# Stage 1 of a fused attention and expert kernel: root steps divided between tiles 2 and 3, one chunk of statistics in another buffer, the first store of turned rows ahead of three loads

## The reference, cut to what matters

```python
mod = (silu(c) @ wmod)                        # six rows of 256: sa, ca, ga, sb, cb, gb
h = layernorm(x) * (1 + ca) + sa              # mean and variance of each token's 256 values
x_in = concat(mem, h)                         # 64 memory rows ahead of 4096 tokens
out_swa = swa(x_in, wq, wk, wv, wo)           # 4 heads, window 128
# loss = 0.5 * sum((mlp(x_in) - out_swa)**2); grads of w1, b1, w2, b2
# new = (1 - alpha) * old - theta * grad
out_mem = mlp(new, x_in)
x = x + ga * (sigmoid(out_swa @ lin1.T) * out_swa + sigmoid(out_mem @ lin2.T) * out_mem)[:, 64:]
h = layernorm(x) * (1 + cb) + sb
x = x + gb * (shared_expert(h) + top8_of_64_experts(h))
```

## Time and profile before

| | before |
|---|---|
| median of three runs | 1840.76 us |
| the profiled execution's own time | 1840.37 us |
| its span | 1838.2 us |
| PE busy | 1794.2 us (98%) |
| DVE busy | 1214.8 us (66%) |
| ACT busy | 947.9 us (52%) |
| POOL busy | 935.5 us (51%) |
| mean granted TensorE clock | 0.993 |

### The profile page before, as it was taken

The page is one execution under the profiler, slowest core; times in us unless marked ns, Lnnn a source line. Parts: engine busy times, 40 slices in busy tenths (PEclk is TensorE's granted clock), DMA queues, the critical chain, the costliest instruction groups (busy, mean ns, idle before and its releaser), DMA issues.

```text
span 1838.2 us, 35720 instructions
## 1 busy us (share of the span) xinstructions
PE 1794.2 (98%) x12168; PEld 1578.6 (86%) x12168; DVE 1214.8 (66%) x2253; ACT 947.9 (52%) x1792; POOL 935.5 (51%) x699
## 2 busy tenths in 40 slices
PE   7999999999999999999999999999999999999995
PEld 5788888888888887788788887889999999999995
DVE  7977777777777776766677668644555555555552
ACT  7666666666666665634545444343444434444341
POOL 6565666656666664046566666554233323332234
PEclk9999999999999999999999999999999999999998
DMA  6211111111111102220111103167898888888884
GB/s 239 69 39 36 38 37 35 38 35 35 55 39 35 39 28 81 70 74 17 47 46 47 47 12 109 39 227 254 291 286 288 283 279 281 289 289 283 284 278 96
DMA packets 141023, 234.16 MB, mean 127 GB/s; under 512 B 24757, under 2 KB 88972, under 8 KB 140817
## 3 DMA queue, kind: packets, MB, share of 16 engines
q1 hardware_dynamic: 116368, 220.50, 35.0%
q0 software_dynamic: 24576, 12.69, 4.6%
HBM read 194.58 MB, written 78.45 MB: 149 GB/s over the span
## 4 chain that ended last, share of the span: by engine, by line
PE 53%; DMA 3%; issue 1%; DVE 1%; POOL 0%; ACT 0%; SPq 0%; POOLq 0%; DVEq 0%; ACTq 0%
PE bank L86 26%; PE bank L2048 22%; PE bank L1312 4%; DMA out_rows<-c_y_rest,c_token_rest 2%; DMA c_w<-in_e1T 1%; PE bank L2270 1%; PE bank L1811 1%; DMA slots<-last_row,last_index 1%; POOL out_rows L2222 0%; POOL slots L2007 0%; PE bank L2281 0%; SPq L2104 0%; DVE c_y_rest L2189 0%; DVE early L1690 0%; POOLq L2356 0%
## 5 line engine op out<-in xcount | busy, mean ns | idle before, releaser
L2048 PE MATMUL bank<-c_xT,c_w 128*128 128x160 f32 x3072 | 429.9, 299 | 3.7 <-DMA c_w<-in_e1T 3.0
L2048 PEld LDWEIGHTS bank<-c_xT,c_w 128*128 128x128 f32 x3072 | 419.3, 190 | 5.0 <-DMA c_w<-in_e1T 3.4
L2007 POOL DMA_INDIRECT slots<-b_row,b_index x224 | 251.2, 1121 | 194.3 <-issue 116.4
L2222 POOL DMA_INDIRECT out_rows<-c_y,c_x x64 | 100.1, 1564 | 376.2 <-DMA out_rows<-c_y_rest,c_token_rest 275.1
L2170 DVE TENSOR_TENSOR c_gT<-bank,c_sil 128x480 f32<-128x480 f32 x128 | 84.2, 658 | 212.0 <-PE bank L2048 212.0
L2138 ACT CAST c_gTs_high<-c_gT 128x384 fp32r<-128x384 f32 x128 | 65.6, 513 | 135.3 <-DVE c_gT L2170 135.3
L2131 ACT ACTIVATE c_sil<-bank 128x480 f32<-128x480 f32 x128 | 73.1, 571 | 110.7 <-PE bank L2048 110.2
L2163 DVE TENSOR_TENSOR c_gTs_low<-c_gT,c_gTs_high 128x384 fp32r<-128x384 f32 x128 | 71.6, 560 | 74.8 <-ACT c_gTs_high L2138 74.8
L485 POOL TENSOR_TENSOR last_row<-last_row,a_e 128x256 f32<-128x256 f32 x33 | 53.5, 1620 | 124.5 <-DVE a_e L783 124.5
L86 PE MATMUL bank<-c_w2s_high,c_gTs_high 128*128 128x256 f32 x384 | 114.0, 297 | 0.9 <-DVE c_gTs_low L2163 0.9
L86 PE MATMUL bank<-c_w2s_high,c_gTs_low 128*128 128x256 f32 x384 | 106.9, 278 | 0.0
(11 more groups left out here) (346 smaller groups left out, 5451.0 us busy)
## 6 DMA issues: line engine op xcount, KB each, us to landing
c_w<-in_e1T SPq DMA_DIRECT2D x64, 1536.0 KB, 7.0
c_w<-in_e2T SPq DMA_DIRECT2D x48, 768.0 KB, 9.0
early<-in_e2T SPq DMA_DIRECT2D x16, 768.0 KB, 8.7
slots<-a_fill SPq DMA_DIRECT2D x16, 642.0 KB, 3.9
c_x<-slots SPq DMA_DIRECT2D x64, 160.5 KB, 8.6
a_x_in<-in_x SPq DMA_DIRECT2D x32, 128.0 KB, 2.0
xT_tiles<-a_xT SPq DMA_DIRECT2D x32, 128.0 KB, 1.7
swaT_tiles<-a_oT SPq DMA_DIRECT2D x32, 128.0 KB
```

What stands on the lines that cost most here:

```text
L2007: pool.indirect_dma_start(out=T["slots"], out_offset=bass.IndirectOffsetOnAxis(ap=index[:, t, k:k + 1], axis=0), in_=row[:, t, :], in_offs ...
L2048: return nc.tensor.matmul(out, lhsT, rhs, start=first, stop=last, skip_group_check=True)
L2222: pool.indirect_dma_start(out=T["out"], out_offset=bass.IndirectOffsetOnAxis(ap=token, axis=0), in_=rows, in_offset=None, bounds_check=las ...
```

## The change

- The wqk load and the cond load change places on SP.
- Chunk 4 goes to raw[2] instead of raw[1], chunk 6 to raw[3] instead of raw[2]; chunks 5, 6 and 7 thus share raw[3].
- SP loads chunk 1 alone before it stores tile 1's turned rows. Then come chunk 2, the two biases, step 1, chunk 3, chunk 4 (after `mod_mm` 3), chunk 5, step 2, chunk 6 (after `stats` 6) and chunk 7 (after `stats` 7), and only then the fills.
- ACT makes dz's high part of tile 0 in tile 1 ahead of h's high part, and no longer waits for five chunks' statistics.
- DVE in tile 1 does grad_z ahead of hidden_low and grad_z_low ahead of statistics(4).
- The twelve root steps of chunks 1 to 7 are cut otherwise: steps 0 to 5 behind statistics(7) in tile 2, steps 6 to 11 in tile 3 behind the reciprocal and the first of four gathers.

```diff
@@ -248,7 +248,7 @@
         wv_raw = h[:, 0:DC * D].rearrange("p (k n) -> p k n", k=DC)
 
         x_pre = [a.rearrange("p (t d) -> p t d", t=TPC)
-                 for a in (dz_raw[1], h_raw[0], h_raw[1], dz_sum[:], raw[1], dz_raw[1], dz_raw[0], dz_raw[1])]
+                 for a in (dz_raw[1], h_raw[0], h_raw[1], dz_sum[:], dz_raw[0], dz_raw[1], dz_raw[1], dz_raw[1])]
 
         def bank(b, n=CH):
             return psum[b][:, 0:n]
@@ -304,8 +304,8 @@
                 sp.dma_start(x_pre[c], x_chunks[c]).then_inc(S(f"x_pre{c}"), 16)
 
             sp.dma_start(x_in[0][P - MEM:P, :], T["mem"]).then_inc(S("mem_in"), 16)
+            sp.dma_start(wqk_raw, T["wqkT"]).then_inc(S("wqk_in"), 16)
             sp.dma_start(cond[:], T["c"]).then_inc(S("cond_in"), 16)
-            sp.dma_start(wqk_raw, T["wqkT"]).then_inc(S("wqk_in"), 16)
             load_chunk(0)
             for k in range(DC):
                 sp.dma_start(dW1T[:, k, :], T["w1T"][:, k, :]).then_inc(S(f"w1_in{k}"), 16)
@@ -325,12 +325,7 @@
             sp.wait_ge(S("xm"), 1)
             sp.dma_start(x_in[0][:], x_rows[P:2 * P, :]).then_inc(S("x_in0"), 16)
             sp.dma_start(dW2[:], T["w2n"]).then_inc(S("w2n_in"), 16)
-            for c in range(1, 4):
-                load_chunk(c)
-            sp.wait_ge(S("stats"), 1)
-            for name, into in (("b2c", b2c), ("b1c", b1c)):
-                sp.dma_start(into[:], T[name]).then_inc(S("small_in"), 16)
-
+            load_chunk(1)
             def step(n, p):
 
                 sp.wait_ge(S("xn"), n)
@@ -356,16 +351,20 @@
                                  fill[0:rows, half, :].unsqueeze(1).to_broadcast([rows, CLEARED, ROW]))\
                         .then_inc(S("slots_out"), 16)
 
+            keep_xT(1)
+            load_chunk(2)
+            for name, into in (("b2c", b2c), ("b1c", b1c)):
+                sp.dma_start(into[:], T[name]).then_inc(S("small_in"), 16)
+            step(1, 1)
+            load_chunk(3)
+            sp.wait_ge(S("mod_mm"), 3)
+            load_chunk(4)
+            sp.wait_ge(S("stats"), 1)
             load_chunk(5)
-            keep_xT(1)
-            sp.wait_ge(S("mod_mm"), 2)
-            load_chunk(4)
-            step(1, 1)
-            sp.wait_ge(S("mod_mm"), 3)
-            load_chunk(6)
             step(2, 0)
-            sp.wait_ge(S("stats"), 6)
-            load_chunk(7)
+            for c in (6, 7):
+                sp.wait_ge(S("stats"), c)
+                load_chunk(c)
             sp.wait_ge(S("fill"), 1)
             for half, rows in enumerate((P, CAP_B)):
                 sp.dma_start(T["out"][TOKENS + half * P:TOKENS + half * P + rows, :], fill[0:rows, half, 0:D])\
@@ -548,7 +547,6 @@
                     wait_past(act, S("dW_mm"), 4 * m - 4 * pm)
                 if not known(m, 1):
                     act.wait_ge(S("mod_mm"), 3)
-                    act.wait_ge(S("stats"), 5)
                 elif not known(m, 2):
                     act.wait_ge(S("stats"), CHUNKS)
                 for g in range(2):
@@ -652,14 +650,13 @@
                     turned(2, 0)
                 elif ahead(n):
                     turned(n + 2, p)
-                if known(n, 3):
+                if known(n, 1) and not (known(n, 2) and not known(n, 3)):
                     dz_high(n - 1, 1 - p)
                 if known(n, 1):
                     hidden_high(n, p)
                 if known(n, 1) and not known(n, 2):
                     act.wait_ge(S("w2n_low"), 4)
                     kept(dW2)
-                    dz_high(0, 0)
                 act.wait_ge(S("swa_mm"), n + 1)
                 wait_past(act, S("eT_mm"), n)
                 act.copy(swa[:], psum[7][:, D:2 * D]).then_inc(S("swa"), 1)
@@ -834,8 +831,6 @@
                     if known(n, 3) and not known(n, 4):
                         grad_z_low(1, 1)
                     turned_error_low(n - 1)
-                    if known(n, 3) and not known(n, 4):
-                        deviations(1, range(1, CHUNKS), range(5))
 
                 seen = slice(P - MEM if first else 0, P)
                 chosen = own[:, seen].unsqueeze(1).to_broadcast([P, DC, P - seen.start])
@@ -860,8 +855,6 @@
                     error_low(0, 0)
                 if known(n, 2) and not known(n, 3):
                     statistics(5)
-                if known(n, 3) and not known(n, 4):
-                    deviations(1, range(1, CHUNKS), range(5, RSQRT_OPS))
                 dve.wait_ge(S("prob_exp"), n + 1)
                 wait_past(dve, S("prob"), n)
                 dve.reciprocal(prec, psums).then_inc(S("prec"), 1)
@@ -876,8 +869,8 @@
                     modulate(1, 1)
                     part_prob(0, 0)
                 elif not known(n, 2):
+                    grad_z(0)
                     hidden_low(0, 0)
-                    grad_z(0)
                     hidden(1)
                     modulate(3, 1)
                     part_prob(1, 1)
@@ -886,7 +879,12 @@
                         dve.wait_ge(S("kept"), 1)
                     elif not known(n, 4):
                         dve.wait_ge(S("kept"), 2)
-                    gather_dW(n - 2, dW1T if p else dW2, (1, 2, 3, 4))
+                    if known(n, 3) and not known(n, 4):
+                        gather_dW(1, dW1T, (1, 2, 3, 4), (0,))
+                        deviations(1, range(1, CHUNKS), range(6, RSQRT_OPS))
+                        gather_dW(1, dW1T, (1, 2, 3, 4), (1, 2, 3))
+                    else:
+                        gather_dW(n - 2, dW1T if p else dW2, (1, 2, 3, 4))
                     if ahead(n):
                         modulate(n + 2, p)
                     part_prob(n, p)
@@ -920,10 +918,11 @@
                     dve.wait_ge(S("b2row"), 1)
                     dve.wait_ge(S("rates"), 1)
                 elif not known(n, 2):
+                    grad_z_low(0, 0)
                     statistics(4)
-                    grad_z_low(0, 0)
                 elif not known(n, 3):
                     statistics(7)
+                    deviations(1, range(1, CHUNKS), range(6))
                 else:
                     grad_z_low(n - 1, 1 - p)
```

## The result

The changed kernel takes 1846.47 us (median of 7 runs, 1844.04 to 1848.97) where the kernel before took 1840.92 beside it (7 runs, 1838.13 to 1841.71). The ratio is 1.0031, 95% interval [1.0019, 1.0043]: slower by 5.5 us. The forecast was 1841.9, a loss of 1.5 us in the profiled execution, with a range of 1837.4 to 1845.5; the median lies 1.0 us above the range. A later repeat (f1_again) gave 1845.54 us, ratio 1.0028 [1.0017, 1.0039]. The profiled execution took 1844.72 us (span 1842.5), 4.35 more than that of before.

A forecast was written before the change was run, and what follows sets the result against it. PE, busy 98% of the span, bounds the kernel, with holes only up to tile 3. DVE's +3.6 us, less 1.9 gained earlier and 0.2 of PE slack, gives +1.5 on 1840.4: 1841.9 us, range 1837.4 to 1845.5.

The forecast's parts named there:

- Up to chunk 6's statistics everything is thus 0.3 + 1.2 + 0.4 = 1.9 us earlier: Start to tile 2: gains of start, store and tile 1's reordering carry through, so these statistics start at 67.5 us.
- from reciprocal to hT low: Tile 3 on DVE: 8.1 us instead of 6.15, from seven added short steps and POOL's L459; hT low at 95.6.
- The new wait: Tile 2: DVE waits 3.5 us for chunk 7, issued only after chunk 6's statistics and landing 4.4 us later.
- the first meeting: Tile 3: DVE's dz low stands behind POOL's dz sum, costing 2.3 us, and is ready at 83.9 us.
- signs of being right: Expected in the profile: L509 without store wait, DMA wait in tile 2, root steps at 0.22 us, L770 behind POOL's L440.
- Start: First loads: wqk ahead of cond gains 0.3 us, between a gain of 0.6 and a loss of 0.6.
- Store: Tile 1: the first store, ahead of three loads, lands by 27 us, so PE gains its 1.2 us wait.
- The swap: Tile 1: grad_z ahead of hidden_low speeds POOL's product, but PE still needs h: 0, up to 0.9 us.
- (a): Tile 3: DVE gets its place ahead of POOL, no meeting, 2.4 us less: 1839.5 us; chance 0.20.
- (c): Tiles 2 and 3: quick chunk 7 load (3.1 us) and no meeting, 1838.2 us, at best 1837.4; chance 0.14.
- (b): Tile 2: chunk 7 lands late with the fills, up to 8.0 us after issue, 1845.5 us; chance 0.16.
- (d): Tile 1: the store still lands after chunk 2, losing its 1.2 us gain, 1843.1 us; chance 0.08.

The follow-up runs named there:

- f1_again: The changed kernel once more, unaltered, as a repeat: 1845.54 us, ratio 1.0028 to the kernel before.
- e9: The kernel before with only SP's new order (first store ahead of the chunk loads, fills last), chunks alternating between two buffers: 1837.94 us, ratio 0.9982.
- e8: e4 with all root steps back at their places in the kernel before, ahead of tile 3's picks and reciprocal: 1838.11 us, ratio 0.9987.
- e4: The changed kernel with chunk 6 back in dz_raw[0], hidden_low ahead of grad_z in tile 1 and cond loaded ahead of wqk: 1838.24 us, ratio 0.9990.
- f2: The changed kernel with PE's idle times in tiles 1 and 3 filled with products nobody reads: 1843.3 us, ratio 1.0014.
- e2: The changed kernel with hidden_low ahead of grad_z again in tile 1: 1844.14 us, ratio 1.0022.
- f4: The changed kernel with root steps 6 to 11 and the offset ahead of tile 3's reciprocal: 1843.19 us, ratio 1.0014.
- e5: e4 with root steps 6 to 11 and the offset ahead of tile 3's reciprocal instead of between its gathers: 1835.67 us, ratio 0.9970.
- f3: The kernel before with one number changed, chunk 7's load issued when chunk 6's statistics are done, not chunk 5's: 1842.36 us, ratio 1.0013.
- e7: The changed kernel with POOL's dz sum of tile 1 made to wait for dz low, so DVE goes first: 1845.03 us, ratio 1.0022.

## Why the prediction was wrong

Two steps failed. "Up to chunk 6's statistics everything is thus 0.3 + 1.2 + 0.4 = 1.9 us earlier": in the profiled execution it was 0.2 later, by the order of the first loads and by a fall of PE's clock. And "from reciprocal to hT low" took 10.0 us instead of 8.1, by a second meeting with POOL. The new wait and the first meeting, the core of the forecast, came out. All its signs of being right came too: none of them looked at when chunk 6's statistics begin or at what stands behind the reciprocal.

Point by point, with the steps as the prediction has them:

- **Start, "I take a gain of 0.3": wrong in sign.** S is 0.67 longer. Among profiles of kernels with the same start S spreads over 1.3 to 1.6 us; over the ten with cond behind wqk its mean is 21.4, over the eight with cond first 20.9: a cost of about 0.5. I had named this case ("a loss of 0.6 if cond's delay passes through") and chose the other, because DVE's statistics row 7.25 seemed to be the next step. It was not: q low waits for PE's products, and they begin at 6.14 behind ACT (5.79 before, behind the load of wqk).
- **Store, 1.2, and dz_high, 0.4: nearly right.** e9's A is 1.4 shorter, and e8 and e4, which have the other edits of tile 1 but the swap, are 0.25 and 0.44 shorter still.
- **The swap, "0, and up to 0.9": the order costs 0, its effect on the clock was missing.** With it and no long fall A is 32.67 (f1) and 32.68 (f2), without it 32.71 (e2). But it moves PE's idle time, to 1.05 and 1.85 us where the earlier trace rows and the trace of before have 1.72, 0.78 and 0.89. In all eight profiles with the swap and without filling in tile 1 the clock fell there, in five of them to 0.50 for all of 45 to 50 us, and then A is 33.7 to 34.1; of the eight without the swap four show a fall and none so long a one. In the profiled execution that took 1.3 of the 1.6 us. That the swap is what makes the fall long rests on these counts; f1 has the same two idle times (1.06 and 1.86) and a short fall.
- **So "up to chunk 6's statistics everything is 1.9 us earlier" failed:** they start at 69.62 against the earlier trace rows 69.40, 2.1 us later than the 67.5 on which the rest is built. This is the larger part of the error. In f1, with its short fall, they start at 68.95, 1.4 us later than forecast; there the fall at 100 us adds 1.6 instead.
- **The new wait, 3.5 with a landing of 4.4: right.** 3.23 and 4.25.
- **The meeting, dz low ready at s + 6.9: right.** 82.18 + 3.47 is s + 6.7, with s = 78.99 for the second e instruction. The forecast says that it starts late; the profile shows it begun beside the sum and drawn out. L118, from whose row I took the price, reads one tensor and not two: its 2.33 us beside 2.41 show that such a step meets POOL as well.
- **The reciprocal, s + 10.5, "from picks to reciprocal 3.3": nearly.** 89.11 is s + 10.1.
- **"From reciprocal to hT low 8.1": mis-sized, it is 10.0.** The term "0.5 us because POOL's L459 holds the first of them" came out (L121 took 0.65), but the next of POOL's operations, L474, began 0.07 us ahead of the offset and held it for 2.2 us more. I had followed POOL only one instruction far. f4 measures it: 1.8 us of C.
- **Sum.** hT low came at 99.09 instead of 95.6, 3.5 us late. By terms: 2.1 from the late arrival (1.0 of it the start, 1.2 the clock in A, rounded), -0.1 up to s, -0.4 from s to the reciprocal, +1.9 behind it. For PE +1.5 was predicted and +5.1 measured at error (4), 3.6 more.
- **The rivals.** (a) and (c) did not come: POOL won the place. (b) priced a late chunk 7 at 1845.5; the time came near that, but its mechanism did not come, as the landing was 4.25. (d) is excluded by the row of L508. That two 0.2-us steps can each be the one that meets POOL, and that idle time can slow what follows it, stood in no rival.

The Trainium skill ("SBUF — State Buffer", SBUF: two separate sides) says that an instruction of DVE with two SBUF inputs and one of GpSimd that reads SBUF exclude each other, the first to start keeping the ports. The meetings here of DVE steps with two inputs agree: 2.87 beside 2.56, 2.38 beside 2.40, 2.35 beside 2.41 us. The prediction used the rule, but for one meeting of two; L118 with its one input is not a case of it.

The Trainium skill ("TensorE: Matmul & The Clock Gate", Part 1: The HAM clock gate (the "warmup" mystery)) says that TensorE's clock is halved when the engine is not active enough and restored by activity. The levels 1.00 and 0.50 and the filled kernels agree; that the same wait ends in a fall in one execution and not in another no sentence of mine had allowed for.

## What to carry to other kernels

Follow each short two-operand step of DVE against all of POOL's instructions of its stretch, not the next one alone, and put such steps where POOL is idle: seven steps of 0.19 us took DVE 1.5 us in one place (80.50 to 82.02, e5) and 4.2 in the other (89.79 to 93.97, the changed kernel). When an edit moves two things, test them one by one: here one half of the split gained 3.3 us of C and the other lost 2.6. When waits are removed ahead of PE, read the granted clock behind those that are left, in more than one execution, since a fall can take back what the edit gave. Two chunks that share a buffer tie a load to the reader of the one before; a landing of 4.3 us then stands on the path, 2 us of loss in the kernel before (f3) and over 5 with the other edits.

## What the runs showed of the hardware

- A DMA of 1 KB issued behind one of 512 KB on the same queue was ready later: cond for ACT at 3.36 to 3.47 us when first (eight profiles), at 5.45 to 6.13 when second (ten).
- A DVE step of 0.18 or 0.19 us that came right behind the start of one of POOL's operations of 2.4 us stood for 2.3 to 2.4 us (L118 in before and e8, L718 in the changed kernel, L123 and L122 in e7).
- The granted clock of a nearly full PE fell to 0.50 after idle stretches of 1 to 2 us, for up to 7 us, but not each time: the changed kernel's two idle stretches in tile 1 brought 0.50 for all of 45 to 50 us in one execution and 0.67 in the other. In the kernel before it was 1.00 from 20 to 120 us, in two kernels with one edit each it fell there twice, and their medians did not change. A fall where another engine sets the end (80 to 88 us) cost nothing; the one at 100 us, about 3.4 us long, cost 1.6.
- Two executions of the changed kernel of the same length (1844.72 and 1844.74 us) lost their time in different tiles: A and C were 34.01 and 26.13 in the one, 32.67 and 27.77 in the other. At error (4) the second was 1.0 us behind the first, so that a microsecond of such a table need not reach the end.
